# A first attention's row maxima turned by TensorE instead of VectorE, and a reordered start

## The reference, cut to what matters

```python
x = x + attention0(layernorm(x)); x = x + ffn0(layernorm(x))
x = x + attention1(layernorm(x)); x = x + ffn1(layernorm(x))

# attention0: 8 heads of 64, keys and values from one latent of 64
q = (x @ Wq.T).reshape(b, t, 8, 64)
kv_latent = x @ Wkv_down.T
k = (kv_latent @ Wk_up.T).reshape(b, t, 8, 64)
v = (kv_latent @ Wv_up.T).reshape(b, t, 8, 64)
attn = softmax(q @ k * 64 ** -0.5)
out = (attn @ v).reshape(b, t, 512) @ Wo.T
```

## Time and profile before

| | us |
|---|---|
| median of 3 runs | 2359.58 (2354.79 to 2359.61) |
| the profiled execution | 2357.26 |
| its span | 2355.5 |
| TensorE busy in the span | 2291.2 |
| VectorE / ScalarE / GpSimd busy | 1372.4 / 1462.7 / 1054.6 |
| first scores of unit 0 | at 39.13 |
| a plain turn (maxima at 578.07 and at 582.00) | 3.9 |
| first product of the second part | at 744.43 |

### The profile page before, as it was taken

The page is one execution under the profiler, slowest core; times in us unless marked ns, Lnnn a source line. Parts: engine busy times, 40 slices in busy tenths (PEclk is TensorE's granted clock), DMA queues, the critical chain, the costliest instruction groups (busy, mean ns, idle before and its releaser), DMA issues.

```text
span 2355.5 us, 39469 instructions
## 1 busy us (share of the span) xinstructions
PE 2291.2 (97%) x14889; PEld 1413.7 (60%) x14889; DVE 1372.4 (58%) x2155; ACT 1462.7 (62%) x2017; POOL 1054.6 (45%) x674
## 2 busy tenths in 40 slices
PE   7999999999998999999999999999999999999999
PEld 5455455455555888888888886444444444444688
DVE  5655756666753133222222224889889889899364
ACT  5777677777764344444444443677778778778643
POOL 1676876876875355645645745130000000000354
PEclk8999999999999999999999999999999999999999
DMA  2112222212203456555555556343333333332232
GB/s 62 64 55 93 81 63 83 90 64 82 89 28 132 143 175 200 180 170 197 192 170 192 179 179 186 102 108 76 90 81 66 91 78 67 94 82 49 75 114 78
DMA packets 158379, 259.09 MB, mean 110 GB/s; under 512 B 38796, under 2 KB 98828, under 8 KB 157836
## 3 DMA queue, kind: packets, MB, share of 16 engines
q1 hardware_dynamic: 158188, 256.53, 36.1%
HBM read 206.52 MB, written 60.68 MB: 113 GB/s over the span
## 4 chain that ended last, share of the span: by engine, by line
PE 63%; DMA 2%; ACT 2%; DVE 1%; issue 1%; SPq 1%; POOL 0%; ACTq 0%
PE m_R L130 47%; PE m_O L130 11%; PE m_X L130 4%; DMA m_K<-bounce_k 1%; ACT m_P L1786 1%; PE m_X L227 1%; DMA bounce_k<-m_comp 1%; DVE m_mraw L1938 0%; ACT m_OS L1793 0%; SPq L1644 0%; PE m_X L2152 0%; PE m_R L227 0%; ACT m_comp L1806 0%; DVE m_ln_stat L184 0%; POOL m_act1l L2043 0%
## 5 line engine op out<-in xcount | busy, mean ns | idle before, releaser
L1938 DVE TENSOR_REDUCE m_mraw<-m_R 128x2 f32<-128x1024 f32 x512 | 622.9, 1222 | 68.4 <-PE m_R L130 56.3
L1786 ACT ACTIVATE m_P<-m_R 128x1024 f32<-128x1024 f32 x512 | 524.5, 1027 | 149.4 <-PE m_R L130 149.2
L130 PE MATMUL m_O<-m_P,m_V 128*17 128x256 f32 x4096 | 329.4, 393 | 4.5 <-ACT m_P L1786 2.6
L771 DVE CUSTOM_DVE_ANT_0 a_excess<-a_X,a_excess 128x512 f32<-128x512 f32 x256 | 166.4, 688 | 179.9 <-PE a_X L130 178.1
L942 POOL TENSOR_TENSOR a_accp<-a_accp,a_P 128x1024 f32<-128x1024 f32 x96 | 258.0, 2687 | 20.9 <-ACT a_P L624 12.1
L624 ACT ACTIVATE a_P<-a_S 128x1024 f32<-128x1024 f32 x256 | 250.1, 1041 | 17.1 <-PE a_S L130 17.0
L2043 POOL TENSOR_TENSOR m_act0l<-m_xf,m_act0h 128x512 fp32r<-128x512 f32 x128 | 165.0, 1292 | 209.7 <-ACT m_xf L1848 110.3
L130 PE MATMUL m_R<-m_act0h,wt 128*128 128x512 f32 x640 | 251.4, 393 | 0.0
L130 PE MATMUL m_R<-m_act0l,wt 128*128 128x512 f32 x640 | 250.5, 391 | 0.0
L130 PE MATMUL a_O<-a_P,a_V 128*64 128x512 f32 x1024 | 248.5, 606 | 0.0
L130 PE MATMUL m_R<-m_Q,m_K 64*128 64x512 f32 x800 | 200.2, 497 | 2.3 <-DVE m_mraw L1938 2.0
(11 more groups left out here) (270 smaller groups left out, 4159.9 us busy)
## 6 DMA issues: line engine op xcount, KB each, us to landing
wt<-wcopy SPq DMA_DIRECT2D x176, 512.0 KB, 3.3
m_K<-bounce_k SPq DMA_DIRECT2D x96, 128.0 KB, 5.6
m_ln_x<-x SPq DMA_DIRECT2D x23, 512.0 KB, 4.0
a_tile<-in_L_ffn_tiles SPq DMA_DIRECT2D x22, 512.0 KB, 3.4
wcopy<-in_L_ffn_tiles SPq DMA_DIRECT2D x22, 512.0 KB, 4.9
x<-xres SPq DMA_DIRECT2D x78, 128.0 KB, 1.8
m_Q<-bounce_q SPq DMA_DIRECT2D x150, 64.0 KB, 2.3
xres<-x SPq DMA_DIRECT2D x64, 128.0 KB, 2.9
```

Source lines behind the costliest of these rows:

```text
L130: return pe.eng.matmul(out, lhsT, rhs, start=start, stop=stop, skip_group_check=True)
L771: dve.eng.tensor_tensor_reduce(excess[:, h, :], bank(key), excess[:, h, :], 1.0, LOWEST, ALU.add, ALU.max, mraw[u % 2][:, q, h:h + 1]).the ...
L1786: act.eng.activation(P[h % 4][:, :, :], pair(key)[:, :, :], ACT.Exp, scale=SCALE).then_inc(R.free(key))
L1938: dve.eng.tensor_reduce(mraw[u % 2][:, at, :], pair(key)[:, :, :], AX.X, ALU.max).then_inc(R.free(key))
```

## The change

TensorE turns the negated maxima: a product of `mneg` with the identity, 8 rows by 128 columns, into one more user of the ring (`("rows", u)`), which ScalarE copies to `mrow`, now 8 partitions by 128. The rows of `M` then come from it with 2 DMAs for each unit instead of 8. In the loop, product and copy stand in turn (u, 2) for unit u + 1, behind that turn's second maxima product on TensorE and behind its two exponentials on ScalarE. VectorE's transpose and one memset are gone.

`out_low` moves from GpSimd to VectorE for all tiles, behind `reduce` of its turn. The norm's steps begin one turn earlier and the offset has a turn of its own (n = 13), one before the first scaling.

At the start the turned input of sequence 0 is rounded before the folded query weights; query(1) comes after the first two steps of maxima; `values(0)` is made in four pieces, after steps 1, 3, 5 and 7, into `psO` (free until the first weighted sums) instead of a ring bank; `differ(0, 1)` comes after step 9, the maxima of unit 0 are turned after step 10, and `differ(0, 0)` comes last. Small tiles and semaphores change to suit.

```diff
-        at = (8, 9, 10, 11, 12, 14, 15, 16, 17, 18, 19, 20, 21)
-        return (b + 1, at.index(n)) if n in at and (b + 1 < B or at.index(n) in (0, 1, 4, 5, 6, 7, 8)) else None
+        at = (7, 8, 9, 10, 11, 13, 14, 15, 16, 17, 18, 19, 20, 21)
+        return (b + 1, at.index(n)) if n in at and (b + 1 < B or at.index(n) in (0, 1, 4, 5, 6, 7, 8, 9)) else None
...
-        out += [("q", 0), ("halves", 0), ("q", 1), ("values", 0)]
-        for n in range(2 * AHEAD):
-            out += [("max", n, h) for h in range(NH)] if n % 2 else []
-            out += [("differ", 0, 1), ("differ", 0, 0)] if n == NT - 1 else []
+        out += [("q", 0), ("halves", 0)]
+        for n in range(1, 2 * AHEAD, 2):
+            out += ([("rows", 0)] if n == 2 * AHEAD - 1 else []) + [("max", n, h) for h in range(NH)]
+            out += [("q", 1)] if n == 1 else [("differ", 0, 1)] if n == NT + 1 else []
...
+            out += [("rows", rows_at(u, j))] if rows_at(u, j) else []
...
-                sp.wait_ge(s_turned, u + 1)
+                sp.wait_ge(*X.emptied(("rows", u)))
...
                 for h in range(NH):
-                    to = M[u % 3][64 * h:64 * h + 1, :].rearrange("o (q i r) -> o i q r", q=4, i=4)
-                    for i in range(4):
-                        part = slice(32 * i + 4 * h, 32 * i + 4 * h + 4)
-                        sp.eng.dma_start(f32(to[:, i, :, :]), f32(mrow[u % 2][part, :])).then_inc(s_rows[u % 3], 16)
+                    sp.eng.dma_start(f32(M[u % 3][64 * h:64 * h + 1, :]), f32(mrow[u % 2][4 * h:4 * h + 4, :])).then_inc(s_rows[u % 3], 16)
...
+            def keep_rows(u):
+                key = ("rows", u)
+                act.wait_ge(*X.filled(key))
+                if u >= 2:
+                    act.wait_ge(s_rows[(u - 2) % 3], 32 * ((u - 2) // 3 + 1))
+                act.eng.activation(mrow[u % 2][:, :], bank(key)[0:NH * 4, 0:128], ACT.Copy).then_inc(X.free(key))
...
+            for i in range(4):
+                norm.turn_act(act, 0, i % 2, i // 2)
             act.wait_ge(s_prod, 1)
             for i in range(2):
                 for k in range(2):
                     to = wq[0][:, k, :].rearrange("p (g i n) -> p g i n", g=NG, i=2)[:, :, i, :]
                     act.eng.activation(to, psS[i][:, k, 0:256].rearrange("p (g n) -> p g n", g=NG), ACT.Copy).then_inc(s_whi)
...
-            for i in range(4):
-                norm.turn_act(act, 0, i % 2, i // 2)
             for half in range(2):
                 latent_high(0, half)
-            for u in range(2):
-                query_high(u)
-            keep_values(0)
+            query_high(0)
+
+            def first_values():
+                act.wait_ge(s_first, 1)
+                act.eng.activation(V[0][:, :, :], psO[:, :].rearrange("p (t n) -> p t n", t=NT), ACT.Copy).then_inc(s_kept)
...
             for n in range(0, 2 * AHEAD, 2):
                 for h in range(NH):
                     surplus(n, h)
-                if n == NT - 2:
-                    for half in (1, 0):
-                        differ_high(0, half)
+                if n == 0:
+                    query_high(1)
+                if n == NT:
+                    first_values()
+                    differ_high(0, 1)
+            keep_rows(0)
+            differ_high(0, 0)
             for m, (u, j) in enumerate(turns()):
...
+                if rows_at(u, j):
+                    keep_rows(rows_at(u, j))
...
                     halved = mraw[u % 2][:, :, :].rearrange("p q (h k) -> p h q k", k=1)
-                    dve.eng.tensor_reduce(mneg[:, 0:NH * 4].rearrange("p (h q) -> p h q", h=NH), halved, AX.X, ALU.max, negate=True).then_inc(s_max)
-                    if u >= 2:
-                        dve.wait_ge(s_rows[(u - 2) % 3], 128 * ((u - 2) // 3 + 1))
-                    dve.wait_ge(s_max, u + 1)
-                    dve.eng.transpose(f32(mrow[u % 2][:, :]), f32(mneg[:, :])).then_inc(s_turned)
+                    dve.eng.tensor_reduce(mneg[:, :, :], halved, AX.X, ALU.max, negate=True).then_inc(s_max)
...
             norm.scale(dve, 0, NT // 2, NT)
+            for i in range(4):
+                norm.turn_dve(dve, 0, i % 2, i // 2)
             for i in range(2):
...
-            for i in range(4):
-                norm.turn_dve(dve, 0, i % 2, i // 2)
             for half in range(2):
                 latent_low(0, half)
+            keep_halves(0)
             query_low(0)
-            keep_halves(0)
-            query_low(1)
...
             for n in range(1, 2 * AHEAD, 2):
                 reduce(n)
-                if n == NT - 1:
-                    for half in (1, 0):
-                        differ_low(0, half)
+                if n == 1:
+                    query_low(1)
+                if n == NT + 1:
+                    differ_low(0, 1)
+            differ_low(0, 0)
...
+                if out_at(u, j):
+                    out_low(*out_at(u, j))
...
-            def out_low(b, t):
-                cols = slice(128 * t, 128 * t + 128)
-                pool.wait_ge(s_oh, out_index(b, t) + 1)
-                pool.eng.tensor_tensor(osp[t % 2][1][:, :, :], ON[b % 2][:, :, cols], f32(osp[t % 2][0][:, :, :]), ALU.subtract).then_inc(s_ol)
-
             for m, (u, j) in enumerate(turns()):
-                if out_at(u, j):
-                    out_low(*out_at(u, j))
...
+            def max_rows(u):
+                key = ("rows", u)
+                pe.wait_free(X, key)
+                pe.wait_ge(s_max, u + 1)
+                mm(pe, bank(key)[0:NH * 4, 0:128], mneg[:, :, :].rearrange("p h q -> p (h q)"), identr[:, :]).then_inc(X.full(key))
...
-                pe.wait_ge(s_rows[u % 3], 128 * (u // 3 + 1))
+                pe.wait_ge(s_rows[u % 3], 32 * (u // 3 + 1))
...
-                pe.wait_ge(*X.emptied(("values", b)))
+                pe.wait_ge(*(X.emptied(("values", b)) if b else (s_kept, 1)))
...
             key_halves(0)
-            query(1)
-            pe.wait_ge(s_identr, 1)
-            values(0)
+
+            def first_values(t):
+                for half in range(2):
+                    pe.wait_ge(*X.emptied(("latent", 0, half)))
+                for i in (t, t + 1):
+                    terms = [(k[0][0:64, 128 * i:128 * i + 128], identr[0:64, 0:64]) for k in (Kh, Kl)]
+                    ins = products(pe, psO[:, 64 * i:64 * i + 64], terms)
+                if t == NT - 2:
+                    ins.then_inc(s_first)
+
             for n in range(2 * AHEAD):
                 maxima(n)
-                if n == NT - 1:
-                    for half in (1, 0):
-                        differ(0, half)
-            pe.wait_ge(s_fill, 8)
+                if n == 1:
+                    query(1)
+                if n in (1, 3, 5, 7):
+                    first_values(n - 1)
+                if n == NT + 1:
+                    differ(0, 1)
+                if n == 2 * AHEAD - 2:
+                    max_rows(0)
+            differ(0, 0)
+            pe.wait_ge(s_fill, 7)
...
```

More of the change, by code:

```diff
@@ L381, in attention_a @@
         accd, accp = [p.sb(f"accd{i}", [128, NH, 512]) for i in range(2)], p.sb("accp", [128, NH, 512])
-        mrow = [p.sb(f"mrow{i}", [128, 32], F32R) for i in range(2)]
+        mrow = [p.sb(f"mrow{i}", [NH * 4, 128], F32R) for i in range(2)]
         total = p.sb("total", [128, 256])
@@ L392, in attention_a @@
         mraw = [p.sb(f"mraw{i}", [128, NT // 2, NH]) for i in range(2)]
-        mneg = p.sb("mneg", [128, 32], F32R)
+        mneg = p.sb("mneg", [128, NH, 4], F32R)
         norm.small_tiles(p)
-        lows = p.sb("lows", [128, LOWS + 2])
-        low_all, low_top = lows[:, LOWS:LOWS + 1], lows[0:1, LOWS + 1:LOWS + 2]
+        lows, low_all, low_top = p.sb("lows", [128, LOWS]), p.sb("low_all", [128, 1]), p.sb("low_top", [1, 1])
         s_copy, s_tile, s_tile_hi, s_low = p.sem("copy"), p.sem("tile"), p.sem("tile_hi"), p.sem("low")
@@ L405, in attention_a @@
         s_lathi, s_qhi, s_max = p.sem("lathi"), p.sem("qhi"), p.sem("max")
-        s_rows, s_turned = [p.sem(f"rows{i}") for i in range(3)], p.sem("turned")
+        s_first, s_kept = p.sem("first"), p.sem("kept")
+        s_rows = [p.sem(f"rows{i}") for i in range(3)]
         s_scores, s_exp, s_pv, s_os = p.sem("scores"), p.sem("exp"), p.sem("pv"), p.sem("os")
@@ L411, in attention_a @@
         s_rinv = [p.sem(f"rinv{i}") for i in range(2)]
-        s_on, s_oh, s_ol, s_old = p.sem("on"), p.sem("oh"), p.sem("ol"), p.sem("old")
+        s_on, s_oh, s_ol = p.sem("on"), p.sem("oh"), p.sem("ol")
         s_xres, s_store = [p.sem(f"xres{i}") for i in range(4)], [p.sem(f"store{i}") for i in range(4)]
@@ L459, in low_done @@
         def low_done(b, t):
-            return (s_old, t - 3) if b == B - 1 and t >= 4 else (s_ol, out_index(b, t) + 1)
+            return s_ol, out_index(b, t) + 1
         def sync(eng):
@@ L580, in latent_high @@
                     act.wait_ge(s_scores, NT * UB * (b - 1))
-                    act.wait_ge(*X.filled(("values", b - 2)))
```

(11 more changed lines are left out.)

12 lines of the change are left out of this document (7 added, 5 removed).

## The result

The change is faster: 2341.39 us at the median of 5 runs (2332.85 to 2346.39) against 2354.79 of before (5 runs, 2352.12 to 2359.61), ratio 0.9933 with a 95% interval of 0.9915 to 0.9951. Run again beside 11 runs of before it gave 2339.52 against 2357.94, ratio 0.9921 (0.9907 to 0.9935).

What follows compares the result with a forecast made beforehand. The kernel was taken to be bound by TensorE's own work and the gaps in it. Savings of -17.2 us and costs of +9.8 net -7.4; from the profiled 2357.26, moved halfway to the median, 2351 us, range 2343 to 2360.

Steps and rivals of the forecast that it cites:

- rows: Row DMAs in the loop, two per unit: all seven gaps before the scores close, -6.0 us.
- remainders: Output tiles' remainders, moved from GpSimd to VectorE: most of 3.9 us of TensorE gaps go, -3.5 us.
- column sums: TensorE's column sums in the loop: reciprocal sums land 2 to 4 us sooner, so waits shrink, -2.7 us.
- product: TensorE's 31 added turning products in the loop, at 0.22 us each: +6.8 us (3.4 to 14).
- ring: Turning product as one more bank user: waits for its bank and the turned input's first, +3.0 us (1 to 7).
- norm: Norm's offset a turn earlier: ScalarE finds it done before the first scaling, -3.0 us.
- start: New order and two DMAs at the start: first scores near 37.1 instead of 39.1, -2.0 us (-4 to 0).
- rival (a): In the loop, waits change names: TensorE reaches ScalarE's or VectorE's banks before they are free; 2358.5 us, chance 0.27.
- signs of being right: No scores' waits for row DMAs, no offset or column-sum waits, product 0.2 us, first scores near 37, second part near 737.
- (b): Slower by ScalarE's queue: rows late behind two exponentials, deciding at 2.1 us more than counted; 2372 us, chance 0.04.
- (c): TensorE's work only: product costs 0.45 us and nothing but the rows' wait goes; 2365 us, chance 0.05.
- (d): More gain than counted: product at 0.11 us, no ring waits, clock kept at the start; 2343 us, chance 0.12.

Runs made afterwards that it cites:

- turn_again: Second run of the kernel before with only the turning changed (TensorE product, ScalarE copy, two row DMAs per unit): 2339.08 us, 0.9924 of before.
- eight_dmas: Changed kernel with eight row DMAs for each unit instead of two: 2401.83 us, 1.0194 of before.
- scale_late: Kernel before with only GpSimd's scale_out moved behind the adds of its turn: 2339.82 us, 0.9925 of before.
- four single edits: Kernel before with the turning, the remainders' move, the norm's steps or the start's order alone: 2339.40, 2351.27, 2354.93, 2353.89 us.
- after_again: Changed kernel run once more, unaltered, beside the turning alone on the same chip: 2339.52 us, 0.9921 of before.
- norm_only: Kernel before with only the norm's steps one turn earlier and the offset in its own turn: 2354.93 us, 0.9990 of before.
- turn_only: First run of the kernel before with only the turning changed (TensorE product, ScalarE copy, two row DMAs per unit): 2339.40 us, 0.9922 of before.

## Why the prediction was right or wrong

**What bounds the kernel:** right. The difference in the first attention is in gaps between TensorE's products, in the product added, and in short stretches at half clock behind gaps. By kind of turn, the forecast and the profiled pair (us):

| | terms of the sum | forecast | measured |
|---|---|---|---|
| turns 0 | rows, remainders | -9.5 | -13.3 |
| turns 1 | column sums | -2.7 | -3.8 |
| turns 2 | product, ring | +9.8 | +8.5 |
| turns 3 | norm | -3.0 | -8.6 |
| start | start | -2.0 | -2.65 |
| behind unit 29 | none | 0 | -1.95 |
| sum | | -7.4 | -21.8 |

The turning alone (`turn_again`) has -13.3, -3.9, +6.0 and -7.4 in the first four rows.

**The rows.** Right in mechanism (though the copy has 8 rows and not 32, and takes 0.25 us): no unit waits, and the tightest has 4.4 us between copy and scores, where 2.35 were counted to the landing. That landing isn't seen where nobody waits for it; in `eight_dmas` the waiting scores began 1.1 to 1.2 us after the last issue in most units, which makes some 2.5 here (an estimate), but 2.1 to 3.1 us after it in units 24 to 29. The size was off. The sum took 6.0, TensorE's idle time; the seven turns 0 that had these waits became shorter by 0.6 to 1.8 each, 7.8 together. A gap costs more than its idle time, here about 0.25 us each: a product of the scores is recorded with 0.40 us, though the next starts 0.23 after it, so that the first part of a gap doesn't show as idle.

**The reciprocal sums and GpSimd.** Here the prediction failed. It had the right chain, the reciprocal sums "2 to 4 us sooner" (their issue: 2.3, from 9.5 to 7.2), but its term for it, -2.7, priced one kind of wait, and gave the remainders' 3.5 and the norm's 3.0 to other parts of the change. By its terms the turning alone would be 1.1 us slower in the loop (-6.0 - 2.7 + 6.8 + 3.0); measured, it is 17.0 and 18.9 us faster. It closes the remainders' gaps without touching them, and turns (3,3) and (11,3), in which ScalarE's banks come late behind the norm's offset, become 1.2 and 2.7 us shorter in `turn_again`. The queues form a ring: the column sums wait for GpSimd's adds, `move_sums` for the column sums, the rows and then the reciprocal sums stand behind `move_sums` on SyncE, and GpSimd's adds stand behind the reciprocal sums. The seven rows' waits of before stand in units where SyncE began the rows 2.7 to 3.8 us after the start of turn 2; the earliest begin at 0.2 (some late units, 5, 14 and 22, have longer turns and don't wait). Six DMAs fewer loosen the ring in one place, `scale_late` in another, and either edit alone gives 17 to 19 us. That the parts' gains can't be added is shown by the four single edits (26 us) and by `after_again` beside `turn_again`. The remainders' move, norm and start were priced at 3.5, 3.0 and 2.0; beside the turning they come to no measurable time, and in the profiles only the start brings something on top of it.

**The norm.** 3.0 was taken, the idle time, and the turns (3,3) and (11,3) became 1.5 and 2.9 shorter in the profile. The larger gap cost more than that: behind its 1.84 us before's clock falls to half for a while, and the next turn, (12,0), is 0.8 us longer too.

```profile
292.00:296.00 4.00, 4.00 (x16) 1.69 (x14) 2.84 (x5) 3.70 (x6) 2.03 (x2) 0.59 0.34 99
```

(The number behind the busy times, 0.59, is the granted clock.) But the turning alone takes most of these gaps, as said, and the norm's own steps bring new waits: `norm_only` shows 1.4 us, inside its noise, and turns 2 longer by 6.0, which is what rival (a) described, for this part alone.

**The product.** 0.22 us was taken, 0.15 measured: 4.7 us for 31 instead of 6.8. "Sixty-four columns at 0.11 look like four passes" was wrong; each further product of 128 columns takes 0.06. The 0.11 of the small products was probably that of their weights: each loads 128 columns of them, recorded with 0.19 us, the turning product 8, recorded with 0.09. No run tried it. By the Trainium skill ("TensorE: Matmul & The Clock Gate", back-to-back issue gap) it would be 81 ns with the weight load. The 0.15 measured lies as far above that as below the row that was chosen, and the 0.06 of a further product lies below both.

**The ring:** +3.0 forecast, some 1.6 measured where it stands alone (turns 2 of `turn_again` are 6.0 longer, less 29 x 0.15). The wait at the first turned bank came as described, 0.75 us in each of four units, where 0.3 to 0.7 stood before. The changed kernel has 2.5 more in its turns 2, from waits of 0.2 to 0.9 for VectorE in units 2, 11, 19 and 27. They aren't the ring's: `turn_again` has none of them, and `norm_only`, without a product, has those of 11, 19 and 27.

**The start:** -2.0 forecast; first scores 2.2 earlier, and unit 1 begins 2.65 earlier. The term was right within a few tenths to there, by the steps given: copy at 34.0 (34.4), scores at 36.9 (37.1). The half clock stays over the first scores (0.50 from 37 to 40 us in both profiles) but ends sooner: from 40 to 44 it is 1.00, before has 0.56 there.

**Signs and rivals.** The signs of being right came, but for the second part's first product: 722.6, where 737 was named. Of the signs of being wrong one came in part, turns with TensorE waiting for `mraw`. (b) and (c) are excluded by 4.8 us between copy and scores, and by the product's 0.15. The decision point of (b), 2.1 us more than counted, fits `eight_dmas`: 3.75 us more, and the kernel is slower than before. (d), 2343, came nearest, but by luck: of its reasons (product at 0.11, no ring waits, the clock) none holds in full, and they are worth a few us of the 14 by which the sum fell short in the profiled pair.

## What to carry to other kernels

Follow a late transfer around the queues before pricing it: where A's queue waits for B, B's for C and C's for A, one edit can take out nearly all of the loop's waits, and the next ones then find little, as here. Price a gap by the length of the turn with and without it, not by the idle time in front of an instruction. An engine that waits for data that only one of its instructions needs should do the others first; that edit moved one call and was worth as much as the whole change. The length of such a wait says little, though: 161 us of it cost the changed kernel nothing that taking it out gave back.

## What the runs showed of the hardware

Executions of one program differed by 13.5 us, and the granted clock goes with it: the changed kernel's five runs have 2332.85 us at a mean clock of 0.996, 2346.39 at 0.991. Two profiles of the same program show a place. The second part's wait for its keys, and a stretch behind one of them, in the profile of 2332.85 us:

```profile
PE m_R L130 <- DMA m_K<-bounce_k: 1.0, 1, 1.0
```

```profile
1660.00:1664.00 4.00, 4.00 (x41) 1.66 (x37) 4.00 (x4) 3.49 (x5) 0.73 (x1) 1.00 0.04 12
```

and in that of `after_again` (span 2338.1 us), with another such stretch at 2020:

```profile
PE m_R L130 <- DMA m_K<-bounce_k: 4.9, 3, 2.0
```

```profile
1660.00:1664.00 4.00, 3.74 (x27) 1.42 (x27) 2.46 (x3) 1.62 (x4) 0.10 (x1) 0.75 0.08 25
...
2020.00:2024.00 4.00, 3.96 (x25) 1.28 (x27) 2.56 (x3) 1.08 (x2) 0.00 (x0) 0.57 0.08 25
```

Behind the wait of 1.0 us the clock stays full (the columns are busy times and counts of five engines, then the clock). Behind those of 1.9 and 2.0 it is granted at its half level, 1.2 GHz, for part of the next 4 to 8 us. The length of the one wait doesn't decide it: in `turn_again` a wait of 2.3 at 1662 leaves the clock at 1.00, in `turn_only` it is 0.70 behind one of 1.3 at 2024.

The second part took 1608.4 us in the one and 1614.8 in the other. Over all profiles it took 1611.4 to 1616.1 where the waits for the keys summed to 3.0 us or more, and 1607.3 to 1611.1 elsewhere. All seven profiles of the first kind are of kernels that turn on TensorE with two DMAs, which have one other profile, that of 2332.85 us; none of the seven profiles with VectorE's transpose is among them. So the kernels with the new turning lose, by their profiles, some 4 us of their gain again in the second part. This may be part of why the changed kernel, 8 us ahead of `scale_late` when the second part starts (722.62 against 730.88), has the same median as that kernel. Each kernel has one or two profiles, and why the waits for the keys are longer stays open; no kernel was made to try it.
